# Score matmuls in row tiles with masks moved off TensorE, one ring of four PSUM banks, and value products issued for two steps together

## The chip, the cores and the metric

One core of one Trainium2 chip. The metric is device time in microseconds (us) of one execution, as the median of a few runs; lower is better.

## What is computed

Input x is 4 batches x 1024 tokens x 128 features, all fp32. Two blocks follow each other, both with 16 heads of 8 features:

```python
x = x + layernorm(attn(layernorm(x)))          # causal attention with ALiBi bias
x = x + layernorm(ffn(layernorm(x)))           # full attention, then a mixture of experts

def attn(x, Wq, bq, Wk, bk, Wv, bv, Wo, bo):
    q, k, v = heads(x @ Wq + bq), heads(x @ Wk + bk), heads(x @ Wv + bv)   # 16 heads x 8
    scores = einsum('bhqd,bhkd->bhqk', q, k) * 8 ** -0.5
    scores = scores + slopes[:, None, None] * (qpos - kpos)
    scores = where(kpos <= qpos, scores, -inf)
    return einsum('bhqk,bhkd->bqhd', softmax(scores), v) @ Wo + bo

def ffn(x, ...):
    x = x + layernorm(attention(x), ln1)       # no bias on the scores, no mask
    return x + layernorm(moe(x), ln2)          # 8 experts, top 2, hidden 512, gelu
```

## The kernel before, in words

`build` runs five stages: a row pass `first` (layernorm, transposes, values), the causal attention `at1`, a row pass `second`, the full attention `at2`, and `tail` (output projection, norms, experts). Both attentions are the function `attention` (L206) with another `Plan` (L56). The change lies there; in `build` only constants change.

**Slots.** An attention works in 16 slots, one for a batch and a group of four heads. The four heads lie side by side in the 128 partitions, 32 rows each: 24 rows hold the 8 features three times over (high and low parts, since fp32r keeps fewer bits), the rest bias and maximum rows. `fq` is the query side. `km` is the key side with four copies, one for each head, in which the rows of the other three heads are zero, so that a 128-row matmul gives one head's scores.

**Streams of a slot** (names as in the code):
- `proj`, 4 a slot, three slots ahead: three matmuls (a fourth for the causal bias) into the bank `misc`; ScalarE reads it into `u` (L404); GpSimd splits it (`hi` L556, `part` L559, then `fq` L564 or `fk` L567 and the four masked copies `km` L569). In the first slot VectorE does this.
- `a`: scores with queries on the partitions, only for each row's maximum. A chunk is 128 queries by up to 512 keys (L333), for several heads at once where the causal width is under 512. In the causal attention a chunk on the diagonal gets a second matmul that adds the mask (L337). VectorE reduces the bank by maximum (L466). Three banks.
- `m`, `mtr`: VectorE joins the maxima (L474 to L481), TensorE transposes them into `misc` (L346), VectorE adds them to the queries, `fqm` (L486).
- `b`: scores with keys on the partitions, maximum taken off (L360), with a mask matmul on the diagonal (L363). ScalarE takes exp into `probs` (L415). Three banks.
- `pv`: four matmuls with 32 columns each, one a head, side by side in the array, accumulate values and row sums in the bank `pv` (L378); `oev` copies it out (L420), `otr` transposes it back (L385), VectorE divides (L492, L494).

**Order.** One list, made by `Plan.body` for a slot, is walked by all engines. It has a step for each quad (512 queries x 128 keys x 4 heads): 12 quads in the causal attention, 16 in the other. A step holds four `b`, about four `a` between them, at times a `proj`, `mtr` or `otr`, and the `pv` of the quad before. TensorE issues in this order, so whatever it waits for holds everything behind it. `a` works a slot ahead of `b`. The loop runs over three batches with four slots in its body; four slots and a prologue are written out.

## Time and profile before

| | |
|---|---|
| median of 3 runs | 2289.69 us (2287.66 to 2295.19) |
| profiled execution, first to last instruction | 2287.5 us; the lowest run is 0.2 us above it |
| TensorE busy | 2102.9 us (92%), 11100 matmuls |
| VectorE busy | 1671.8 us (73%) |
| ScalarE busy | 1373.5 us (60%) |
| GpSimd busy | 977.3 us (43%) |
| mean granted TensorE clock | 0.959 |

A granted clock of 1.00 is 2.4 GHz, 0.50 is 1.2 GHz. Busy time of TensorE is the union of matmul spans; matmuls are pipelined, so a span (0.4 us for 512 columns) is longer than the distance between two starts. Distances between starts are what counts.

### The profile page before, as it was taken

The numbers are of one execution on the slowest core, as the hardware profiler recorded it, in microseconds if no ns is written. First come the engines' busy times: TensorE is split into PE (matmuls) and PEld (weight loads), VectorE is DVE, ScalarE is ACT, GpSimd is POOL, SyncE is SP. The second block draws the span as 40 slices with busy tenths as digits, with TensorE's granted clock in tenths as the row PEclk, the third lists the DMA queues.
The fourth block names the chain that finished last, engine by engine and source line by source line (L and its number), as shares of the span: only waits on it lengthen the run. The fifth ranks groups of instructions, "written<-read, shape, count | busy, mean of one in ns | idle before, by whom it ended". The sixth has DMA issues, their size and how long they took to land. (4 is left out here: it accounts for less than half of the span.)

```text
span 2287.5 us, 41083 instructions
## 1 busy us (share of the span) xinstructions
PE 2102.9 (92%) x11100; PEld 1223.1 (53%) x11100; DVE 1671.8 (73%) x3157; ACT 1373.5 (60%) x2647; POOL 977.3 (43%) x744
## 2 busy tenths in 40 slices
PE   5899999999999679999999999999993999999996
PEld 4455555555554534555555555555531666666664
DVE  5766667666672787777777777778822899998986
ACT  4266566666666616666666666666672655555654
POOL 3665464553610355333333333342002466565554
PEclk7799999999999679999999999999996999999998
DMA  2000000000000300000000000000001100000000
GB/s 59 1 2 1 3 1 1 2 2 1 1 1 2 110 0 1 2 1 1 2 1 1 2 1 1 1 1 1 1 1 61 51 19 19 2 19 19 19 10 10
DMA packets 27508, 24.96 MB, mean 11 GB/s; under 512 B 2409, under 2 KB 21110, under 8 KB 27282
## 3 DMA queue, kind: packets, MB, share of 16 engines
q1 hardware_dynamic: 26400, 21.91, 3.2%
q8 instruction: 103, 1.69, 0.3%
q14 instruction: 123, 1.01, 0.2%
q10 hardware_dynamic: 882, 0.36, 0.1%
HBM read 13.87 MB, written 6.29 MB: 9 GB/s over the span
## 5 line engine op out<-in xcount | busy, mean ns | idle before, releaser
L466 DVE TENSOR_REDUCE at_mx<-at_a 128x1 f32<-128x512 f32 (+3 forms) x1632 | 1010.8, 675 | 358.7 <-PE at_a L333 249.5
L415 ACT ACTIVATE at_probs<-at_b 128x512 f32<-128x512 f32 (+3 forms) x1792 | 888.6, 558 | 474.0 <-PE at_b L360 292.7
L333 PE MATMUL at_a<-at_km,at_fq 128*128 128x512 f32 (+1 forms) x1632 | 704.8, 439 | 20.4 <-DVE at_mx L466 9.8
L360 PE MATMUL at_b<-at_fqm,at_km 128*128 128x512 f32 (+3 forms) x1792 | 710.8, 404 | 11.4 <-ACT at_probs L415 7.6
L333 PEld LDWEIGHTS at_a<-at_km,at_fq 128*128 128x128 f32 x1632 | 316.3, 194 | 290.0 <-DVE at_mx L466 224.4
L360 PEld LDWEIGHTS at_b<-at_fqm,at_km 128*128 128x128 f32 x1792 | 339.8, 191 | 205.5 <-ACT at_probs L415 120.3
L378 PE MATMUL at_pv<-at_probs,at_vst 128*32 128x512 f32 (+3 forms) x3584 | 437.9, 561 | 1.5 <-ACT at_probs L415 1.5
L556 POOL TENSOR_TENSOR at_hi<-at_u,split_sign 128x512 fp32r<-128x512 f32 x120 | 124.9, 1041 | 441.1 <-ACT at_u L404 306.5
L1172 ACT ACTIVATE t_hid<-t_bank_h,b1t 128x512 f32<-128x512 f32 x256 | 174.3, 689 | 195.9 <-DVE t_hid_lo L1306 113.1
L1306 DVE TENSOR_TENSOR t_hid_lo<-t_hid,t_hid_hi 128x512 fp32r<-128x512 f32 x256 | 225.6, 917 | 15.0 <-ACT t_hid_hi L1179 11.8
L569 POOL TENSOR_TENSOR at_km<-at_fk,head_mask 128x2048 fp32r<-128x2048 f32 x60 | 216.1, 3602 | 11.2 <-POOL at_fk L567 11.0
L1340 POOL TENSOR_TENSOR t_hid_hi<-t_hid,pow_cols 128x512 fp32r<-128x512 f32 x112 | 141.1, 1275 | 129.6 <-ACT t_hid L1172 129.0
L404 ACT ACTIVATE at_u<-at_misc,bias 128x512 f32<-128x512 f32 x128 | 88.2, 689 | 124.7 <-PE at_misc L203 58.0
L526 POOL COPY at_vst<-tokens 128x256 f32 (+1 forms) x32 | 13.0, 405 | 328.5 <-PE at_pv L378 328.2
L201 PE MATMUL t_bank_y<-t_hid_hi,t_w2hi 128*128 128x512 f32 x256 | 106.6, 416 | 31.3 <-DVE t_weighed L1315 26.8
L559 POOL TENSOR_TENSOR at_part<-at_hi,split_sign 128x512 f32<-128x512 f32 x120 | 125.0, 1042 | 21.4 <-POOL at_hi L556 21.4
L378 PEld LDWEIGHTS at_pv<-at_probs,at_vst 128*32 128x32 f32 x3584 | 70.6, 108 | 117.1 <-ACT at_probs L415 85.1
L363 PE MATMUL at_b<-ident,causal_mask 128*128 128x128 bf16 x512 | 117.8, 232 | 0.0
L203 PE MATMUL t_bank_y<-t_hid_hi,t_w2lo 128*128 128x512 f32 x256 | 102.2, 399 | 0.0
L202 PE MATMUL t_bank_y<-t_hid_lo,t_w2hi 128*128 128x512 f32 x256 | 101.9, 398 | 0.0
L337 PE MATMUL at_a<-causal_mask,ident 128*128 128x128 bf16 (+2 forms) x352 | 91.7, 260 | 0.0
L564 POOL TENSOR_TENSOR at_fq<-at_part,at_u 128x512 fp32r<-128x512 f32 x60 | 77.0, 1284 | 10.7 <-POOL at_part L559 10.7
(211 smaller groups left out, 2410.3 us busy)
## 6 DMA issues: line engine op xcount, KB each, us to landing
t_raw<-L_ffn_W SPq DMA_DIRECT2D x16, 256.0 KB, 3.1
x_first<-L_attn_x SPq DMA_DIRECT2D x4, 512.0 KB, 7.3
second_x_in<-L_attn_x SPq DMA_DIRECT2D x8, 256.0 KB, 3.1
kept<-second_joined SPq DMA_DIRECT2D x8, 256.0 KB, 2.6
kept_u<-second_normed SPq DMA_DIRECT2D x8, 256.0 KB, 2.0
t_heads_in<-tokens SPq DMA_DIRECT2D x8, 256.0 KB, 2.6
t_u_in<-kept_u SPq DMA_DIRECT2D x8, 256.0 KB, 3.1
t_x_in<-kept SPq DMA_DIRECT2D x8, 256.0 KB, 3.1
```

The costliest lines, as they stand in the source:

```text
L333: mm = pe.matmul(scores, fq[g][:, qt * P:(qt + 1) * P], km[g][:, heads[0]:heads[0] + k, kh * HALF:kh * HALF + w], start=True, stop=not dia ...
L360: mm = pe.matmul(out[:, 0:w], km[g][:, j, kt * P:(kt + 1) * P], fqm[g % 2][:, q0:q0 + w], start=True, stop=not diagonal)
L363: mm = pe.matmul(out[:, 0:P], causal_mask[:, :], ident16[:, :], start=False, stop=True)
L378: mm = pe.matmul(pv_bank[HW * j:HW * (j + 1), HALF - w:HALF], vst[g % 2][:, kt, j, :], probs[(n % 2) * GH + j][:, 0:w], start=(kt == 0), s ...
L415: act.activation(probs[(t % 2) * GH + j][:, 0:w], b_bank[n % 3][:, 0:w], ACT.Exp).then_inc(exp_done, 1)
L466: dve.tensor_reduce(mx[:, kh, qt, heads[0]:heads[0] + k], a_bank[n % 3][:, 0:k * w].rearrange("p (k w) -> p k w", k=k), AX.X, ALU.max).the ...
L556: pool.tensor_tensor(hi[:, :], un[:, :], split_sign[:, 2:3].broadcast_to([P, HALF]), ALU.add).then_inc(pool_step, 1)
L559: pool.tensor_tensor(part[:, :], hi[:, :].bitcast(F32), split_sign[:, m:m + 1].broadcast_to([P, HALF]), ALU.mult).then_inc(pool_step, 1)
L569: pool.tensor_tensor(km[g][:, :, half], fk[:, None, :].broadcast_to([P, GH, HALF]), head_mask[:, :, None].broadcast_to([P, GH, HALF]), ALU ...
L1172: act.activation(hid[:, f, :], h_bank[f][:, :], ACT.Gelu, bias=b1t[:, f, e:e + 1]).then_inc(hidden["act"], 1)
L1306: dve.tensor_tensor(hid_lo[e % 2][:, f, :], hid[:, f, :], hid_hi[e % 2][:, f, :].bitcast(F32), ALU.subtract).then_inc(hidden["dve"], 1)
L1340: pool.tensor_tensor(out, a, b, op).then_inc(stage["pool"], 1)
```

## The change

- Instead of four masked copies of the keys there is one, `fk`. A score matmul contracts only the 32 rows of its head, so it uses one of four row groups of the array. `a` and `b` matmuls alternate, and `b` takes the heads in the order 2, 3, 0, 1 (`b_head`), so that neighbours use different row groups.
- The mask matmuls go. In `a`, a chunk is one head; on the diagonal ("ragged": 32 of 48 causal chunks) VectorE adds a row mask and takes the maximum in one call. In `b`, exp runs over unmasked scores, and GpSimd then sets the upper triangle of 4 x 128 columns to zero for the quads on the diagonal; `pv` waits for that.
- `a` has four banks, and `proj`, `otr` and `mtr` use the same ring instead of `misc`.
- `pv` of two quads is issued together, ahead of every second step, from four sets of `probs` instead of two.

```diff
+RING = ("a", "proj", "otr", "mtr")
+A_BANKS = 4
+B_BANKS = 3
+PROBS = 4
...
-                per = max(1, HALF // n)
-                per = 4 if per >= 4 else per
-                for j in range(0, GH, per):
-                    self.chunks.append((qt, kh, list(range(j, j + per)), n))
+                for j in range(GH):
+                    self.chunks.append((qt, kh, j, n))
+
+        self.ragged = [i for i, (qt, kh, j, n) in enumerate(self.chunks) if causal and kh * HALF + n == (qt + 1) * P]
...
-        o0 = self.half_end[0] + 3 - self.lead
+        o0 = self.half_end[0] + 1
...
         for i in range(self.nq):
+
+            for p in (i - 1, i) if i % 2 else ():
+                out.append(("pv", 0, p))
+                if p in self.half_end:
+                    out.append(("oev", 0, self.half_end.index(p)))
             q = i + self.lead
...
-            dp, p = (ds, q - 1) if q else (0, self.nq - 1)
-            if dp == 0 or do_a1:
-                out.append(("pv", dp, p))
-                if p in self.half_end:
-                    out.append(("oev", dp, self.half_end.index(p)))
         return out
+
+    def places(self, steps):
+
+
+        order = [step for step in steps if step[0] in RING]
+        return {step: place for place, step in enumerate(order)}
...
+def b_head(n):
+
+
+    return (n + 2) % GH
...
@@ TensorE @@
+                def bank_free(step):
+
+                    place = places[step] - A_BANKS
...
-                        mm = pe.matmul(scores, fq[g][:, qt * P:(qt + 1) * P],
-                                       km[g][:, heads[0]:heads[0] + k, kh * HALF:kh * HALF + w],
-                                       start=True, stop=not diagonal)
-                        if diagonal:
-                            mm = pe.matmul(scores[:, :, w - P:w], ident16[:, :],
-                                           causal_mask[:, None, :].broadcast_to([P, k, P]),
-                                           start=False, stop=True)
+                        rows = slice(HW * j, HW * (j + 1))
+                        mm = pe.matmul(misc[:, 0:w], fq[g][rows, qt * P:(qt + 1) * P],
+                                       fk[g][rows, kh * HALF:kh * HALF + w],
+                                       start=True, stop=True)
...
-                        mm = pe.matmul(out[:, 0:w], km[g][:, j, kt * P:(kt + 1) * P],
-                                       fqm[g % 2][:, q0:q0 + w], start=True, stop=not diagonal)
-                        if diagonal:
-                            mm = pe.matmul(out[:, 0:P], causal_mask[:, :], ident16[:, :],
-                                           start=False, stop=True)
+                        out = b_bank[n % B_BANKS]
+                        rows = slice(HW * j, HW * (j + 1))
+                        mm = pe.matmul(out[:, 0:w], fk[g][rows, kt * P:(kt + 1) * P],
+                                       fqm[g % 2][rows, q0:q0 + w], start=True, stop=True)
...
+                        if n in plan.diagonals:
+                            done(pe, masked, len(plan.diagonals), s, plan.diagonals.index(n))
...
@@ ScalarE @@
-                        if j == 0:
-                            done(act, pv_done, NQ, s, t - 2)
+                        if n % GH == 0:
+                            done(act, pv_done, NQ, s, t - PROBS)
...
@@ VectorE @@
+                        if n in plan.ragged:
+                            ragged = plan.ragged.index(n)
+                            if ragged >= 2:
+                                done(dve, a_read, NA, s, plan.ragged[ragged - 2])
+                            dve.sem_inc(dve_passed, 1)
+                            dve.tensor_tensor_reduce(scrap[ragged % 2][:, 0:w], scores, causal_rows[:, HALF - w:HALF], 1.0,
+                                                     -3.0e38, ALU.add, ALU.max,
+                                                     mx[:, kh, qt, j:j + 1]).then_inc(a_read, 1)
+                        else:
+                            dve.tensor_reduce(mx[:, kh, qt, j:j + 1], scores, AX.X, ALU.max).then_inc(a_read, 1)
...
@@ GpSimd @@
+                    if what == "b" and n % GH == GH - 1 and n // GH in plan.diagonals:
+                        await_(exp_done, NB, s, n)
+                        block_ = probs[n // GH % PROBS][:, :, 0:P]
+                        pool.affine_select(block_, block_, [[0, GH], [1, P]], ALU.is_ge, 0.0, base=0,
+                                           channel_multiplier=-1).then_inc(masked, 1)
...
-                        pool.tensor_tensor(fk[:, :], part[:, :], un[:, :], ALU.add).then_inc(pool_step, 1)
-                        await_(pool_step, count, s, step + 2)
-                        pool.tensor_tensor(km[g][:, :, half],
-                                           fk[:, None, :].broadcast_to([P, GH, HALF]),
-                                           head_mask[:, :, None].broadcast_to([P, GH, HALF]),
-                                           ALU.mult).then_inc(split_done, 1)
+                    dst = fk if m else fq
+                    pool.tensor_tensor(dst[g][:, half], part[:, :], un[:, :], ALU.add).then_inc(split_done, 1)
```

How this moves the instructions. First TensorE in `at2`, in the loop, around a value product; "ISA" stands for a register or wait instruction. Before:

```order
L333 MATMUL at_a<-at_km,at_fq 128x512
L265 ISA
L360 MATMUL at_b<-at_fqm,at_km 128x512
L265 ISA
L378 MATMUL at_pv<-at_probs,at_vst 32x512 x4
L265 ISA
L333 MATMUL at_a<-at_km,at_fq 128x512
L265 ISA
L360 MATMUL at_b<-at_fqm,at_km 128x512
```

and now:

```order
L367 MATMUL at_a<-at_fk,at_fq 128x512
L289 ISA
L390 MATMUL at_b<-at_fqm,at_fk 128x512
L289 ISA
L407 MATMUL at_pv<-at_probs,at_vst 32x512 x4
L289 ISA
L407 MATMUL at_pv<-at_probs,at_vst 32x512 x4
L289 ISA
L367 MATMUL at_a<-at_fk,at_fq 128x512
L289 ISA
L390 MATMUL at_b<-at_fqm,at_fk 128x512
```

Two groups of value products stand in a row, and the next such pair comes two steps later.

VectorE in `at1`, in the loop, among the `a` reductions. Before, three chunks, the middle one of four heads:

```order
L466 TENSOR_REDUCE at_mx<-at_a 128x1
L265 ISA
L466 TENSOR_REDUCE at_mx<-at_a 128x4
L265 ISA
L466 TENSOR_REDUCE at_mx<-at_a 128x1
```

and now, a full chunk and a ragged one with its two instructions at L497 (the second writes the maximum, `at_mx`):

```order
L501 TENSOR_REDUCE at_mx<-at_a 128x1
L289 ISA x2
L497 ISA at_scrap,at_mx<-at_a,causal_rows 128x256
L497 ISA at_mx 128x1
L289 ISA x2
L497 ISA at_scrap,at_mx<-at_a,causal_rows 128x256
```

A diagonal chunk has become one chunk a head, each with one instruction more.

GpSimd in `at1`, in the loop, from the staging of the values. Before:

```order
L526 COPY at_vst<-tokens 128x32x8
L265 ISA x3
L556 TENSOR_TENSOR at_hi<-at_u,split_sign 128x512
L265 ISA
L559 TENSOR_TENSOR at_part<-at_hi,split_sign 128x512
L265 ISA
L567 TENSOR_TENSOR at_fk<-at_part,at_u 128x512
L265 ISA
L569 TENSOR_TENSOR at_km<-at_fk,head_mask 128x4x512
```

and now:

```order
L562 COPY at_vst<-tokens 128x32x8
L289 ISA
L580 AFFINE_SELECT at_probs<-at_probs 128x4x128
L289 ISA
L580 AFFINE_SELECT at_probs<-at_probs 128x4x128
L289 ISA x3
L597 TENSOR_TENSOR at_hi<-at_u,split_sign 128x512
L289 ISA
L600 TENSOR_TENSOR at_part<-at_hi,split_sign 128x512
L289 ISA
L605 TENSOR_TENSOR at_fk<-at_part,at_u 128x512
```

The product for `km` is gone, and masks of the probabilities stand in front of and between the splits.

## Rows read from the trace of the kernel before

**Rows 1.** Windows of `at2`: busy us and count of each engine, clock, DMA share, GB/s
```profile
1000.00:1200.00 200.00, 197.66 (x1034) 106.78 (x1031) 154.51 (x270) 135.36 (x254) 74.86 (x54) 0.99 0.01 2
```
**Rows 2.** Timeline, GpSimd, L526, once a slot: start us, duration us, instruction, idle before
```profile
187.86 0.40 POOL L526 COPY at_vst<-tokens 128x256 f32 x1 [5.98 <-PE at_pv L378]
228.51 0.40 POOL L526 COPY at_vst<-tokens 128x256 f32 x1 [6.00 <-PE at_pv L378]
...
1200.20 0.40 POOL L526 COPY at_vst<-tokens 128x256 f32 x1 [12.55 <-PE at_pv L378]
1254.28 0.40 POOL L526 COPY at_vst<-tokens 128x256 f32 x1 [12.56 <-PE at_pv L378]
```
**Rows 3.** Timeline of `at2`, one step and an output piece
```profile
1303.41 1.06 PE L378 MATMUL at_pv<-at_probs,at_vst 128*32 128x512 f32 x8
1304.41 0.50 PE L333 MATMUL at_a<-at_km,at_fq 128*128 128x512 f32 x1
...
1304.94 3.08 DVE L466 TENSOR_REDUCE at_mx<-at_a 128x1 f32<-128x512 f32 x5 [0.40 <-PE at_a L333]
...
1305.26 1.58 ACT L415 ACTIVATE at_probs<-at_b 128x512 f32<-128x512 f32 x3 [1.41 <-PE at_b L360]
...
1305.91 0.88 PE L333 MATMUL at_a<-at_km,at_fq 128*128 128x512 f32 x2
...
1306.62 0.39 PE L360 MATMUL at_b<-at_fqm,at_km 128*128 128x512 f32 x1
1306.94 1.06 PE L378 MATMUL at_pv<-at_probs,at_vst 128*32 128x512 f32 x8
...
1309.90 0.60 PE L385 MATMUL at_misc<-ident,at_osb 128*128 128x128 f32 x4
...
1310.87 0.25 DVE L492 RECIPROCAL at_rec<-at_misc 128x16 f32<-128x16 f32 x1
1311.32 0.29 DVE L494 TENSOR_TENSOR tokens<-at_misc,at_rec 128x128 f32 x1 [0.19 <-DVE at_rec L492]
```
**Rows 4.** Timeline of `at1`: the maximum's chain, a masked `b`, a narrow value product
```profile
509.80 0.36 DVE L474 TENSOR_TENSOR at_mfull<-at_mx 128x32 f32<-128x32 f32 x1 [0.32 <-DVE at_mx L466]
...
511.39 1.88 DVE L466 TENSOR_REDUCE at_mx<-at_a 128x4 f32<-128x512 f32 x3
...
516.33 0.48 PE L360 MATMUL at_b<-at_fqm,at_km 128*128 128x512 f32 x1
...
516.69 0.42 PE L333 MATMUL at_a<-at_km,at_fq 128*128 128x384 f32 x1
...
519.28 0.42 PE L378 MATMUL at_pv<-at_probs,at_vst 128*32 128x128 f32 x8
519.63 0.45 PE L360 MATMUL at_b<-at_fqm,at_km 128*128 128x384 f32 x1
```
**Rows 5.** Groups by line and form: count, busy us, mean ns, idle us before
```profile
L466 DVE TENSOR_REDUCE at_mx<-at_a 128x1 f32<-128x512 f32 x1408 | 881.9, 685 | 295.4 <-PE at_a L333 249.5 <-PE at_a L337 44.5 <-issue 0.6
L415 ACT ACTIVATE at_probs<-at_b 128x512 f32<-128x512 f32 x1408 | 744.1, 604 | 346.1 <-PE at_b L360 292.7 <-PE at_b L363 49.3
...
L569 POOL TENSOR_TENSOR at_km<-at_fk,head_mask 128x2048 fp32r<-128x2048 f32 x60 | 216.1, 3602 | 11.2 <-POOL at_fk L567 11.0
...
L556 POOL TENSOR_TENSOR at_hi<-at_u,split_sign 128x512 fp32r<-128x512 f32 x120 | 124.9, 1041 | 441.1 <-ACT at_u L404 306.5 <-PE at_b L360 124.8 <-POOL at_km L569 8.7
...
L466 DVE TENSOR_REDUCE at_mx<-at_a 128x1 f32<-128x384 f32 x128 | 70.4, 557 | 42.7 <-PE at_a L337 39.5
...
L486 DVE TENSOR_TENSOR at_fqm<-at_fq,at_misc 128x512 fp32r<-128x512 f32 x64 | 43.6, 682 | 11.7 <-PE at_misc L346 10.7
```
**Rows 6.** Windows: the prologue of `at2` twice, then the last slot of `at2`
```profile
820.00:830.00 10.00, 9.38 (x22) 4.89 (x21) 9.20 (x17) 1.38 (x2) 4.97 (x4) 0.78 0.01 2
830.00:840.00 10.00, 8.74 (x23) 4.14 (x23) 10.00 (x18) 1.38 (x2) 8.75 (x8) 1.00 0.00 1
...
1700.00:1710.00 10.00, 9.02 (x49) 3.63 (x52) 0.00 (x0) 8.30 (x17) 0.00 (x0) 1.00 0.00 0
```

More of the change, by code:

```diff
@@ L76, in __init__ @@
                 self.quads.append((qh, kt))
+        self.diagonals = [t for t, (qh, kt) in enumerate(self.quads) if causal and kt * P >= qh * HALF]
         self.na = len(self.chunks)
@@ L234, in attention @@
         rec = sb("rec", [P, HQ, GH])
-        a_bank = [bank(f"a{i}") for i in range(3)]
-        b_bank = [bank(f"b{i}") for i in range(3)]
+        a_bank = [bank(f"a{i}") for i in range(A_BANKS)]
+        b_bank = [bank(f"b{i}") for i in range(B_BANKS)]
         pv_bank = bank("pv")
-        misc = bank("misc")
+        in_body = plan.places(plan.body())
+        in_prologue = plan.places(plan.prologue())
+        assert len(in_body) % A_BANKS == 0
         proj_made = sem("proj_made")
@@ L261, in attention @@
         o_done = sem("o_done")
+        masked = sem("masked")
         init = sem("init")
@@ L319, in emit @@
                     elif what == "a":
-                        qt, kh, heads, w = plan.chunks[n]
+                        qt, kh, j, w = plan.chunks[n]
                         _, g = where(b0, g0, ds)
@@ L394, in _, with emit @@
                 act.sem_inc(semaphore, per)
-            def emit(steps, s0, b0, g0):
+            def emit(steps, s0, b0, g0, places, before):
                 for what, ds, n in steps:
@@ L403, in emit @@
                         done(act, split_done, 4, s, n - 2)
+                        misc = a_bank[places[what, ds, n] % A_BANKS]
                         act.activation(u[n % 2][:, :], misc[:, :], ACT.Identity,
@@ L428, in _, with emit @@
                 dve.sem_inc(semaphore, per)
-            def emit(steps, s0, b0, g0):
+            def emit(steps, s0, b0, g0, places, before):
                 for what, ds, n in steps:
@@ L438, in emit @@
                         un = u[n % 2]
-                        own = 5 * h if m else 5 * h + 3
+                        own = 4 * h + 2 * (n % 2)
                         done(dve, proj_read, 4, s, n)
@@ L458, in emit @@
+                        dve.tensor_tensor(dst[g][:, half], part[:, :], un[:, :], ALU.add).then_inc(split_done, 1)
                     elif what == "a":
-                        qt, kh, heads, w = plan.chunks[n]
+                        qt, kh, j, w = plan.chunks[n]
                         done(dve, a_made, NA, s, n)
                         if n == 0:
-                            if steps[0] == ("proj", 0, 0) and type(b0) is int and ds == 0:
+                            if places is in_prologue and ds == 0:
@@ L484, in emit @@
                         done(dve, m_turned, 2, s, n)
+                        misc = a_bank[places[what, ds, n] % A_BANKS]
                         h = slice(n * HALF, (n + 1) * HALF)
@@ L488, in emit @@
                     elif what == "otr":
+                        misc = a_bank[places[what, ds, n] % A_BANKS]
                         turned = misc[:, :].rearrange("p (t j c) -> p t j c", t=HQ, j=GH)
@@ L504, in _ @@
         def _(pool):
-            for semaphore, per in ((split_done, 4), (v_staged, 1)):
-                pool.sem_inc(semaphore, per)
+            for semaphore, per in ((split_done, 4), (v_staged, 1), (masked, len(plan.diagonals))):
+                if per:
+                    pool.sem_inc(semaphore, per)
             pool.memset(mpad[:, :, :], 0.0).then_inc(init, 1)
@@ L527, in stage_values, with emit @@
                                  src.rearrange("p t (j c) -> p t j c", j=GH)).then_inc(v_staged, 1)
-            def emit(steps, s0, b0, g0):
+            def emit(steps, s0, b0, g0, places, before):
                 if steps[0][1] == 0 and steps[0][0] == "proj":
@@ L532, in emit @@
                 else:
-                    if any(k[0] == "pv" and k[1] == 1 for k in steps):
+                    if any(k[0] == "b" and k[1] == 1 for k in steps):
                         b, g = where(b0, g0, 1)
@@ L547, in emit @@
                         first = False
-                    if type(b0) is int and steps[0] == ("proj", 0, 0) and ds == 0:
+                    if places is in_prologue and ds == 0:
                         continue
```

124 lines of the change are left out of this document (56 added, 68 removed).

## The prediction

> **What bounds the kernel now.** I read the page first, then the attention stages by windows (which engine is next), by the one instruction that comes once a slot (its length), and by the timeline of single steps (the distances from which the loops are built). The page puts TensorE at 92% of the span. In a stretch of the second attention it is busy 197.7 of 200 us at a granted clock of 0.99, VectorE 154.5, ScalarE 135.4 [rows 1]: the next engine is only a fifth away.
>
> The length of one pass of the loop (a slot: one batch, four heads) comes from the staging copy on GpSimd, once per slot: 187.86 to 228.51, so 40.65 us in the causal attention, and 1200.20 to 1254.28, so 54.08 us in the other [rows 2]. Each attention has 16 slots, about 650 and 865 us. Everything else (prologues, row passes, expert stage) is changed little.
>
> Timeline of a step [rows 3]. A group of value products of four heads starts at 1303.41, the next score matmul at 1304.41: 1.00 us. With 128 columns instead of 512 the same distance is 0.35 us (519.28 to 519.63, [rows 4]), so a group costs 0.13 us plus 1.69 ns a column. Five reductions in a row last 3.08 us, one alone 0.685 [rows 5]: 0.60 from each to the next. Three exps last 1.58, one 0.604: 0.49. From an `a` matmul's start to its reduction 0.53 us (1304.41 to 1304.94); I take the same from `b` to exp. The fifth `a` of a step starts at 1306.39 (1305.91 + 0.88 - 0.40); the second reduction ended at 1306.22: 0.17 us from a freed bank to its next matmul. The next matmul, the last `b`, follows 0.23 us behind it at 1306.62, the pace of score matmuls of 512 columns; the value products follow 0.32 behind that.
>
> **The change, part by part.** (1) *Masks off TensorE.* 54 per causal slot, 32 behind `b` and 22 behind `a`. A masked 512-column matmul takes 0.36 us to the next instead of 0.23 (516.33 to 516.69, [rows 4]); with 54 of them, 7 us a slot of TensorE. It goes to two places.
>
> (1a) VectorE: each of the 32 ragged chunks of a causal slot becomes a fused add and maximum plus a second instruction that writes the result. Add and maximum should take what the reduction takes: the two-input operation on PSUM for `at_fqm` has the same 682 ns as the reduction's 685 [rows 5]. The second instruction is in no row. Below: nothing, if it hides in the chain. Above: 0.25 us, the reciprocal of 16 elements [rows 3]. The other small operations of this chain stand between these, so I take 0.15. 32 x 0.15 = 4.8 us a slot.
>
> (1b) GpSimd zeroes the upper triangle of 4x128 probabilities for 8 of 12 steps. Bounds: 1.04 us (its cheapest 512-element operation) to 3.6 us (the `at_km` product) [rows 5]. I take 1.3, nearest the first since the element count is that. It runs a step ahead of the value products, so it is hidden; if GpSimd is late the value products wait, and both score streams behind them in TensorE's queue (rival E).
>
> (2) *`at_km` goes*: 3.6 us on GpSimd twice a slot, hidden in the bodies (it idles 441 us before `at_hi` [rows 5]), worth perhaps 8 us in the prologues, where splits are awaited.
>
> (3) *One head a chunk.* The causal slot has 48 chunks instead of 38, same columns. A reduction of 384 columns takes 557 ns against 685 for 512 [rows 5], so 0.13 us less per 128 columns: 0.60, 0.47, 0.34 and 0.22 us for 512 to 128. VectorE, causal slot: 16 full x 0.60 = 9.6; 8 x (0.60+0.47+0.34+0.22) = 13.0; second instructions 4.8. Other work: two `at_fqm` 1.2, the maximum's chain 1.9 (509.80 less its wait to 511.39, [rows 4]), two output pieces of 0.75 (1310.87 to 1311.61, [rows 3]): 4.6. Sum 32.0 us. Other attention: 64 x 0.60 + 4.6 = 43.0 us.
>
> (4) *Row tiles, four banks, value products in pairs.* Neighbouring matmuls now use different rows of the array. If they run side by side, TensorE stops being the bound and the ring of banks is. Follow eight chunks between two pairs of value products. From the start of reduction 4: 0.68 until its bank is free, 0.17 to matmul `a8`, 0.23 to `b8`, 0.32 to the value products, 1.00 + 0.87 for the pair, 0.53 to the next reduction: 3.80 us. VectorE has work for 5 x 0.60 = 3.00 of it. So it starves 0.80 us a pair: 8 x 0.60 + 0.80 = 5.6 us for two steps. ScalarE's loop over three `b` banks is 0.60 + 0.17 + 0.32 + 1.87 + 0.23 + 0.53 = 3.72 against 4 x 0.49: 1.76 idle, 5.68 us a pair. Two loops of equal length. Eight pairs are 44.8; with the 4.6 of other work **49.4 us** against 54.1: 16 x 4.7 = 75 us saved. Causal slot: the value products are 1.65, 0.78, 1.87, 1.87, 1.65 and 0.78 us; the same sum gives starvation of 0.6, 0, 0.8, 0.8, 1.5 (narrow chunks and the maximum's chain stand before it) and 0: 3.7. 32.0 + 3.7 + 0.5 for coupling = **36.2 us** against 40.65: 16 x 4.45 = 71 us.
>
> Tiling is also switched more often: four projections and four groups of transposes a slot now stand among row tiles. In the rows a switch from 128x128 to the 32-column products costs about 0.1 us (0.32 less the last matmul's 0.23), so 8 x 2 x 0.1 = 1.6 us a slot of TensorE's time, inside its slack. The Trainium skill, TensorEngine Tiling (Array Packing), Key Properties, says that changing the mode drains the array; by it alone these switches would speak against the change, and if each cost a whole matmul of 0.5 us they would take 8 us a slot. The measured 0.1 us is what such a drain costs here, and even 8 us would fit under 49.4.
>
> (5) *Last slots.* Slots 15 and 16 have few or no `a`. There a step now takes 2.4 us (49 matmul records in 10 us, 12 a step, [rows 6]). ScalarE's loop without `a8` and `a1` is 5.4 us a pair, 2.7 a step. Some 25 steps x 0.3 = 8 us lost, which cancels (2).
>
> **Sum:** 2287.5 - 75 - 71 = 2141.5. The profiled execution's span is 2287.5; the median of the three runs is 2.2 above it, so about **2144 us** for a run.
>
> **The rivals.**
>
> *B: row tiles don't overlap.* For it: each still loads weights of 128 columns, and every matmul has a wait in front. TensorE: eight pairs of 16 x 0.23 + 1.87 + 0.1, i.e. 8 x 5.65 = 45.2; projections 12 x 0.23 = 2.8; 16 transposes of 0.15 (four last 0.60 [rows 3]), 2.4; switches 1.6: 52.0 us a slot, saving 2.1. Causal slot: 33 us of TensorE, below VectorE but close, so about 37.5, saving 3.1. 16 x 5.2 = 83: **2206 us**. The Trainium skill, TensorE: Matmul & The Clock Gate, "Measured speedup vs the span model", gives 3.07x for four row tiles; by it 16 matmuls would take an estimated 1.2 us instead of 3.7 and B falls, but no run here shows it.
>
> *C: overlap shortens the loops too.* If `b8` runs beside `a8` and a result needs less than 0.53 us, starvation halves to 0.4: 3.2 and 1.8 us a slot less, 16 x 5 = 80: **2064 us**.
>
> *D: the clock falls (slower).* TensorE now pauses for a bank after almost every matmul. The nearest stretch is the prologue of the second attention, where VectorE is the bound: 22 matmuls in 10 us with a granted clock of 0.78, then 23 in the next ten with 1.00 [rows 6]: mixed. At 1.2 GHz a pair of value products lasts 1.74 us more and `b8` 0.2: 1.9 x 8 = 15 us a slot, 64.9 us instead of 54.1; causal, the products' 7.8 us double and part is hidden, some 42: 16 x (10.8 + 1.4) = 195 above now, **2485 us**. It decides from a share of time at 1.2 GHz of 0.43 (146 of 341), a mean clock of about 0.78 over the attention stages. Against it: the value products still fill a third of the time, and 200 us with a loop's end in them keep 0.99 [rows 1]. The Trainium skill, TensorE: Matmul & The Clock Gate, "A second HAM failure mode: psum-queue depth-cycling", tells of just this: short idles between groups that cycle through banks make the clock swing between its levels. The prologue agrees in part.
>
> *E: GpSimd's masks come late.* A split (1.04 + 1.04 + 1.28 us and waits) stands between two masks in steps 6 and 7. If a mask takes 3.6 us, four pairs a slot wait about 1 us: +64, **2208 us**.
>
> **How the numbers follow.** Forecast (A) 0.50, B 0.18, C 0.15, D 0.13, E 0.04. The likeliest gives 2144; its own range is 2067 to 2195 from the second instruction alone (-77 to +51). The range 2050 to 2290 takes in B, E, nearly all of C and the mild part of D, and leaves out some 0.17. A measurement of this kernel can tell 0.3% from no change: 7 us. A, B, C and E are all faster; of D 0.11 is slower by more than that, 0.01 within it and 0.01 faster, and 0.01 of B (some clock lost as well) lies within it: faster 0.87, same 0.02, slower 0.11.
>
> **What would show it.** Staging copies 36.2 and 49.4 us apart; the granted clock at 0.95 or more; VectorE with one wait of about 0.8 us per pair of value products and otherwise busy; matmul starts of an `a` and its neighbour `b` under 0.1 us apart (B: 0.23); the second instruction at 0.15 us; value products waiting on GpSimd nowhere. Copies over 54 us apart with a clock below 0.8 would make D right; a TensorE without pauses and 52 us, B.

## The result and the profile after

The changed kernel took **2540.64 us** (median of 4, 2527.02 to 2551.51) against 2288.68 us for the kernel before, measured beside it: 1.109 times as long, 95% interval 1.104 to 1.114. The forecast was 2144 us and faster. The profiled execution, the fastest of the four, spans 2525.3 us, 237.8 more than before. Ratios here and below are of fast executions alone; one run each of x4, x6 and x9, over 1.5% above the fastest of its kernel, is in the times given for it but not in the ratio.

The windows of the two attentions, of the changed kernel (columns as in [rows 1]: busy us and count of TensorE, its weight loads, VectorE, ScalarE, GpSimd; then the clock):

```profile
250.00:700.00 450.00, 405.36 (x2030) 182.88 (x2029) 254.18 (x822) 217.30 (x495) 174.47 (x194) 0.64 0.01 1
1100.00:1600.00 500.00, 457.72 (x2243) 176.44 (x2247) 331.49 (x586) 287.89 (x555) 110.55 (x104) 0.77 0.01 1
```

The granted clock, 0.99 in [rows 1], is 0.64 in the causal attention and 0.77 in the other. Short windows of the second show which two levels make up the 0.77:

```profile
1370.00:1375.00 5.00, 5.00 (x22) 1.73 (x21) 2.18 (x4) 2.13 (x4) 1.28 (x2) 0.50 0.00 0
1385.00:1390.00 5.00, 4.67 (x29) 2.20 (x29) 4.92 (x9) 4.27 (x9) 1.82 (x2) 1.00 0.01 2
1395.00:1400.00 5.00, 5.00 (x26) 1.23 (x24) 1.52 (x4) 0.14 (x2) 0.00 (x0) 0.50 0.00 0
1410.00:1415.00 5.00, 4.34 (x33) 1.60 (x32) 4.25 (x9) 3.11 (x7) 0.00 (x0) 1.00 0.00 0
```

1.2 GHz and 2.4 GHz alternate. At the low level TensorE is busy for 5.00 of 5 us and VectorE for 2.18 and 1.52, at the high one TensorE for 4.67 and 4.34 and VectorE for 4.92 and 4.25. The staging copies of the changed kernel, one a slot, which answer to [rows 2]:

```profile
397.61 0.40 POOL L562 COPY at_vst<-tokens 128x256 f32 x1
446.18 0.40 POOL L562 COPY at_vst<-tokens 128x256 f32 x1
...
1343.22 0.40 POOL L562 COPY at_vst<-tokens 128x256 f32 x1 [17.88 <-PE at_pv L407]
1407.96 0.40 POOL L562 COPY at_vst<-tokens 128x256 f32 x1 [16.25 <-PE at_pv L407]
1469.32 0.40 POOL L562 COPY at_vst<-tokens 128x256 f32 x1 [16.26 <-PE at_pv L407]
```

The causal slot shown takes 48.6 us (they range from 44.4 to 54.7 in the loop; 40.65 before), one of the other attention 64.7 and 61.4 in turn (54.1 before). From the first to the sixteenth copy the causal attention takes 720.4 us against 627.0, the other 931.9 against 828.3: 93.4 + 103.6 = 197 of the 238 us. Another 11 lie between the attentions and some 31 behind the last copy, where the last slot runs at a clock of 0.70.

The timeline of the changed kernel across a change of the clock (it answers to [rows 3]):

```profile
1404.30 3.35 PE L407 MATMUL at_pv<-at_probs,at_vst 128*32 128x512 f32 x16
...
1407.58 0.50 PE L367 MATMUL at_a<-at_fk,at_fq 32*128 32x512 f32 x1
...
1407.58 0.50 PE L390 MATMUL at_b<-at_fqm,at_fk 32*128 32x512 f32 x1
...
1407.59 0.49 PE L367 MATMUL at_a<-at_fk,at_fq 32*128 32x512 f32 x1
...
1407.59 0.72 PE L390 MATMUL at_b<-at_fqm,at_fk 32*128 32x512 f32 x2
...
1408.11 2.48 DVE L501 TENSOR_REDUCE at_mx<-at_a 128x1 f32<-128x512 f32 x4 [2.18 <-PE at_a L367]
...
1411.81 1.93 PE L407 MATMUL at_pv<-at_probs,at_vst 128*32 128x512 f32 x16
1413.66 0.50 PE L367 MATMUL at_a<-at_fk,at_fq 32*128 32x512 f32 x1
```

Three things are read here. Row tiles do run side by side: four matmuls start within 10 ns. The pair of value products takes 3.28 us at 1.2 GHz (1404.30 to 1407.58) and 1.85 us a loop later at 2.4 GHz, and VectorE stands 2.18 us ahead of its next reduction. And at full clock the loop is nearly the forecast one: 6.08 us from 1407.58 to 1413.66 with four output transposes in it, against 5.6 without.

The groups of the changed kernel that answer to the unknown costs (with [rows 5]):

```profile
L407 PEld LDWEIGHTS at_pv<-at_probs,at_vst 128*32 128x32 f32 x3584 | 123.2, 146 | 315.9 <-issue 221.7 <-ACT at_probs L449 85.3 <-POOL at_probs L580 7.9
L497 DVE CUSTOM_DVE_ANT_0 at_scrap<-at_a,causal_rows 128x512 f32<-128x512 f32 x128 | 81.9, 687 | 65.3 <-PE at_a L367 65.3
L580 POOL TENSOR_SCALAR_AFFINE_SELECT at_probs<-at_probs 128x512 f32<-128x512 f32 x128 | 81.6, 640 | 314.5 <-ACT at_probs L449 314.5
...
L497 DVE DVE_READ_ACCUMULATOR2_ANT at_mx<- 128x1 f32 x512 | 42.4, 83 | 0.0
```

Add and maximum take 687 ns, as the reduction; the second instruction 83 ns, the mask on GpSimd 640 ns. The value products' weight loads wait 7.9 us for it in all.

### The profile page after: what moved, and what is told of

It reads as the page before. It is cut to its first block and busy times, and to the rows that moved or that the text cites. A ratio compares the mean times of both kernels' runs of the same rounds, so it can differ in the third digit from the quotient of the medians.

```text
span 2525.3 us, 41740 instructions
## 1 busy us (share of the span) xinstructions
PE 2210.6 (88%) x10396; PEld 1080.9 (43%) x10396; DVE 1659.5 (66%) x3824; ACT 1329.2 (53%) x2647; POOL 837.5 (33%) x812
## 5 line engine op out<-in xcount | busy, mean ns | idle before, releaser
L501 DVE TENSOR_REDUCE at_mx<-at_a 128x1 f32<-128x512 f32 x1280 | 789.0, 683 | 324.3 <-PE at_a L367 322.7
L390 PE MATMUL at_b<-at_fqm,at_fk 32*128 32x512 f32 (+3 forms) x1792 | 687.2, 547 | 91.5 <-ACT at_probs L449 90.7
L367 PE MATMUL at_a<-at_fk,at_fq 32*128 32x512 f32 (+3 forms) x1792 | 599.5, 533 | 54.0 <-DVE at_mx L501 20.9
L407 PE MATMUL at_pv<-at_probs,at_vst 128*32 128x512 f32 (+3 forms) x3584 | 617.9, 830 | 2.7 <-POOL at_probs L580 2.7
L367 PEld LDWEIGHTS at_a<-at_fk,at_fq 32*128 32x128 f32 x1792 | 269.3, 226 | 397.9 <-issue 206.5
L390 PEld LDWEIGHTS at_b<-at_fqm,at_fk 32*128 32x128 f32 x1792 | 290.9, 219 | 319.8 <-ACT at_probs L449 262.5
L497 DVE CUSTOM_DVE_ANT_0 at_scrap<-at_a,causal_rows 128x384 f32<-128x384 f32 (+3 forms) x512 | 232.9, 488 | 237.5 <-PE at_a L367 229.5
L580 POOL TENSOR_SCALAR_AFFINE_SELECT at_probs<-at_probs 128x512 f32<-128x512 f32 x128 | 81.6, 640 | 314.5 <-ACT at_probs L449 314.5
L438 ACT ACTIVATE at_u<-at_a,bias 128x512 f32<-128x512 f32 x128 | 88.0, 687 | 171.5 <-PE at_a L222 112.3
L220 PE MATMUL at_a<-turned_hi,w_hi 128*128 (+1 forms) x128 | 83.4, 652 | 10.7 <-PEq L642 5.8
```

Source lines behind the costliest of these rows:

```text
L220: pe.matmul(out, a[0], b[0], start=start, stop=False)
L367: mm = pe.matmul(misc[:, 0:w], fq[g][rows, qt * P:(qt + 1) * P], fk[g][rows, kh * HALF:kh * HALF + w], start=True, stop=True)
L390: mm = pe.matmul(out[:, 0:w], fk[g][rows, kt * P:(kt + 1) * P], fqm[g % 2][rows, q0:q0 + w], start=True, stop=True)
L407: mm = pe.matmul(pv_bank[HW * j:HW * (j + 1), HALF - w:HALF], vst[g % 2][:, kt, j, :], probs[n % PROBS][:, j, 0:w], start=(kt == 0), stop= ...
L497: dve.tensor_tensor_reduce(scrap[ragged % 2][:, 0:w], scores, causal_rows[:, HALF - w:HALF], 1.0, -3.0e38, ALU.add, ALU.max, mx[:, kh, qt, ...
L501: dve.tensor_reduce(mx[:, kh, qt, j:j + 1], scores, AX.X, ALU.max).then_inc(a_read, 1)
```

## The experiments

The question was why the clock is low: is it idle time (rival D's reason), or something in the matmuls themselves? In each text below, "Theory" and "Rival" are what was expected before that kernel ran.

**x1_full_rows** and **x4_one_group** change only which rows a score matmul contracts. x1, in the second attention (its scores are sums over four heads, so the attention's values are others):

```diff
-                        rows = slice(HW * j, HW * (j + 1))
+                        rows = slice(HW * j, HW * (j + 1)) if causal else slice(0, P)
```

> The changed kernel, but in the second attention every score matmul contracts all 128 rows of fk and fq (so it sums the scores of four heads; its output is not the reference's). No two score matmuls can then run side by side. The causal attention is unchanged. Theory 1 (the clock falls because a score matmul fills only 32 of 128 rows): granted clock 0.97 or more in the second attention, slot 52 us (eight pairs of 16 x 0.23 + 1.87 + 0.1, plus projections and transposes), total about 2527 - 16 x 11 = 2350. Theory 2 (it falls because overlapped score matmuls leave TensorE idle between banks): the same, since TensorE then has no idle time. Theory 3 (it falls because of the ring or the pairs of value products, whatever the matmuls are): clock stays near 0.79, slot 60 us or more.

x4, in both attentions (every head's scores are taken from the first head's rows):

```diff
-                        rows = slice(HW * j, HW * (j + 1))
+                        rows = slice(0, HW)
```

> The changed kernel, but every score matmul uses rows 0 to 31 (all four heads get the scores of the first; its output is not the reference's). The matmuls still fill 32 rows, but must follow each other, 0.23 us apart, as before the change. Theory 1 (few rows filled): clock stays below 0.85 in both attentions, slots of the second attention 62 us or more. Theory 2 (idle time between banks): clock 0.97 or more, slots of 52 us in the second attention and 38 in the causal one, total about 2220.

x1 took 2353.9 us (2347.11 to 2360.69), 1.029 times the kernel before (1.025 to 1.033). x4's two runs took 2789.75 and 2832.51 us; the first is 1.22 times the kernel before. Windows of x1, then of x4, with two short ones:

```profile
1000.00:1600.00 600.00, 589.29 (x3211) 342.63 (x3212) 475.21 (x840) 413.27 (x792) 155.99 (x146) 0.99 0.01 2
```

```profile
1100.00:1800.00 700.00, 693.37 (x2774) 353.00 (x2771) 422.10 (x723) 372.91 (x682) 132.58 (x125) 0.73 0.00 1
...
1515.00:1530.00 15.00, 15.00 (x87) 7.80 (x79) 11.52 (x19) 10.08 (x19) 5.42 (x5) 1.00 0.00 1
1550.00:1580.00 30.00, 30.00 (x87) 16.71 (x86) 16.04 (x27) 13.47 (x23) 3.35 (x3) 0.50 0.00 0
```

x4 decides against idle time: TensorE works 693.4 of 700 us and the clock is still 0.73. From 1515 to 1530 us it works without a gap at the full clock, and from 1550 to 1580 us, again without a gap, the clock is 0.50. Most slots take 70 to 77 us, as its first theory expected (62 or more). Its score matmuls have the rows of one head; x1, with 128 rows and the same order, ring and pairs, is at 0.99, and its slots are 51.8 to 52.0 us, as expected. The values in x1 and x4 are not the reference's; that they make the difference is unlikely, since x12 below computes the reference with 128 rows and pairs, and is at 0.99 too.

**x13_half_rows** stands between the two: 64 rows in the second attention (sums over two heads).

```diff
-                        rows = slice(HW * j, HW * (j + 1))
+                        rows = slice(HW * j, HW * (j + 1)) if causal else slice(2 * HW * (j // 2), 2 * HW * (j // 2 + 1))
```

> The changed kernel, but the score matmuls of the second attention contract 64 rows (two heads summed), so that they use one of two row groups; everything else, the order and the switches between row tiles and whole-array work too, stays. It stands between the changed kernel (32 rows: slots of 61 to 65 us, granted clock 0.77) and x1_full_rows (128 rows: 52 us, 0.99). Theory 'it is the number of rows at work that sets the clock': the clock lies between, 0.85 to 0.95 in 1100 to 1600 us, slots of 54 to 59 us, total 2410 to 2500. Rival 'it is the switching between row tiles and the whole array, or any row group at all, whatever its height': clock 0.75 to 0.80 and slots of 61 us or more, total about 2540.

One run of 2372.55 us. The same window of x13:

```profile
1100.00:1600.00 500.00, 479.79 (x2722) 219.59 (x2722) 399.89 (x709) 345.24 (x671) 134.22 (x126) 0.99 0.01 2
```

Neither number was right: 64 rows already keep 0.99, with slots of 51.0 us. But the rival falls: alternating row groups, pairs and switches are all there, and the height of a score matmul (with it, how many can run side by side) is what the edit changes against the changed kernel's 0.77. TensorE's pauses are there too, though shorter (479.8 of 500 us busy against 457.7); that pauses are not needed for the low clock was x4's result. These 51.0 us are also what the changed kernel's order gives at full clock, with two row groups side by side instead of four; the forecast was 49.4.

**x6_single** keeps 32 rows and issues the value products one step at a time.

```diff
-            for p in (i - 1, i) if i % 2 else ():
+            for p in (i,):
```

> The changed kernel with one thing undone: value products of one step at a time (those of quad i at the head of step i), instead of pairs every second step. Theory 1 alone (32-row matmuls keep the clock down, the pairs are innocent): clock stays near 0.77 in the second attention, slot 60 us or more. Theory 1 with the pairs (with pairs TensorE has 4 us stretches of row tiles only, and falls there; single value products come every 3 us and keep the clock up, as in the warm slots of x2_row_tiles): clock 0.9 or more in the second attention; ScalarE's loop is 0.60 + 0.17 + 0.32 + 1.00 + 0.23 + 0.53 = 2.85 us a step, slot 16 x 2.85 + 3.3 = 49 us where the clock is full, 49 to 53 on average; causal slot 36 to 41. Total 2140 to 2240, below both kernels.

It took 2373.66 us (2350.72 to 2392.25), ratio 1.040 (1.035 to 1.045). Windows of x6:

```profile
250.00:750.00 500.00, 439.55 (x2287) 174.15 (x2288) 296.53 (x928) 249.07 (x560) 188.47 (x212) 0.63 0.01 1
1000.00:1600.00 600.00, 501.73 (x3316) 184.22 (x3312) 494.52 (x866) 427.81 (x816) 157.94 (x149) 0.98 0.01 2
```

Half as expected. In the loop of the second attention the clock is back at 0.98, with TensorE idle *more* (501.7 of 600 us busy), and slots are 50.0 to 50.4 us: there it takes both the few rows and the pairs to lower it. In the causal attention it stays at 0.63 without any pair, with slots of 44 to 54 us (36 to 41 were expected), and the total is above 2140 to 2240. Why the pairs matter in one attention and not in the other is not shown.

**x2_row_tiles** and **x5_masks_off** each make one half of the change to the kernel before. x2 has the row tiles alone; mask matmuls stay between them:

```diff
-                        mm = pe.matmul(out[:, 0:w], km[g][:, j, kt * P:(kt + 1) * P],
-                                       fqm[g % 2][:, q0:q0 + w], start=True, stop=not diagonal)
+                        rows = slice(HW * j, HW * (j + 1))
+                        mm = pe.matmul(out[:, 0:w], fk[g][rows, kt * P:(kt + 1) * P],
+                                       fqm[g % 2][rows, q0:q0 + w], start=True, stop=not diagonal)
```

> The kernel before with the row tiles alone: one fk, 32-row score matmuls, one head a chunk, heads of b in the order 2, 3, 0, 1; masks stay on TensorE, three banks for each stream, the fourth for misc, value products singly. Theories 1 and 2: the clock falls in the second attention, where no mask matmul fills the array, to 0.7 to 0.85, slot above 54.1 us, about 58. Theory 3 (ring or pairs to blame): clock 0.97 or more there and slots of 50 us or less, since VectorE's 43 us are then the bound with waits for exp.

x2 took 2969.14 us (2958.41 to 2979.87), ratio 1.298 (1.292 to 1.303). Its windows:

```profile
300.00:1400.00 1100.00, 1088.20 (x3774) 456.87 (x3778) 374.27 (x744) 357.73 (x726) 151.86 (x144) 0.53 0.00 1
1500.00:2200.00 700.00, 593.94 (x3458) 229.22 (x3461) 542.98 (x944) 449.76 (x843) 189.98 (x178) 0.91 0.01 1
```

and a piece of its causal timeline:

```profile
702.31 0.58 PE L331 MATMUL at_a<-at_fk,at_fq 32*128 32x256 f32 x1
...
702.82 0.29 PE L335 MATMUL at_a<-causal_mask,ident 128*128 128x128 bf16 x1
...
703.04 0.47 PE L359 MATMUL at_b<-at_fqm,at_fk 32*128 32x128 f32 x1
```

Row tiles without the rest are the worst of all: 84.8 us for most causal slots, 1088 of 1100 us busy at 0.53. Each of the 64 masks of a slot (one for each head here, behind `a` and behind `b`) breaks a run of row tiles, so that little overlaps and every mask brings two switches of the array's shape. In the second attention, which has no masks, slots are 52 us with the clock at 1.00 (1610 to 1662) and 58 where it is lower (0.85 over 1662 to 1720). Neither expectation gave this mixture. It has 32 rows, single value products and a mean clock of 0.91, so single value products do not make the clock safe.

x5 has the masks off TensorE, and 128 rows:

```diff
-                        if diagonal:
-                            mm = pe.matmul(out[:, 0:P], causal_mask[:, :], ident16[:, :],
-                                           start=False, stop=True)
```

> The kernel before with the masks alone moved off TensorE (add and maximum on VectorE with one scrap buffer, zeroing on GpSimd, one head a chunk in the causal attention); 128-row score matmuls on km, three banks, value products singly. Every theory: clock 1.0, second attention unchanged at 54.1 us a slot. Causal slot: 54 masks x 0.13 = 7 us of TensorE gone, but VectorE's 32 us and GpSimd's (splits 15, km 7.2, masks 8 x 0.64) come nearer: 36 to 38 us against 40.65. Total 2289 - 16 x 3.5 = 2230, 2200 to 2260. A slot over 40 us would say that the masks were hidden, or that the value products now wait for GpSimd.

x5 took 2362.78 us (2360.33 to 2364.15), ratio 1.033 (1.031 to 1.034), a miss. Its waits in the causal attention, from 300 to 700 us (waited for: us in total, times, longest):

```profile
POOL at_probs L556 <- ACT at_probs L417: 127.4, 45, 6.1
...
DVE at_scrap L475 <- DVE at_mx L475: 37.7, 192, 0.5
...
PEld at_pv L380 <- POOL at_probs L556: 32.1, 23, 2.9
```

Causal slots go from 40.65 to 44.3 us although 54 mask matmuls are gone from each and only 10 more `a` chunks came. The value products, one step behind exp here, wait for GpSimd's masks (rival E's mechanism), VectorE for its own single scrap buffer, and the clock is 0.91; what each of the three costs is not separated. Even with 128 rows the masks' move was a loss in this order.

**x7_filler** and **x8_single_filler** try to buy the clock back: a matmul over 128 rows ahead of every second `b`, overwritten by that `b`; x8 has single value products as well.

```diff
+                        if n % 2 == 0:
+                            pe.matmul(out[:, 0:w], fk[g][:, kt * P:(kt + 1) * P],
+                                      fqm[g % 2][:, q0:q0 + w], start=True, stop=True)
```

> The changed kernel with more work: in front of every second b matmul, a full 128-row matmul into the same bank, which the real one then overwrites. If the low clock is what costs, more work makes it faster: clock 0.95 or more, pairs of steps 5.6 to 6.2 us instead of 7.7 (a filler costs 0.23 us and two switches of tiling), slot of the second attention 48 to 53, causal 40, total 2180 to 2300. If the time goes to something else (ring, GpSimd, switches), the fillers only add: 4 x 0.5 = 2 us a pair, slot 75 us, total 2800.

> x6_single and x7_filler together. Theory 1: clock 0.98 in both attentions; TensorE per step 1.0 + 2 x 0.5 + 8 matmuls of 0.1, under 3 us, so the slots are 50 us and 38, total 2150 to 2230. If x6_single alone already has the full clock, the fillers only cost and this one is slower than x6_single by 2 us a slot or more.

x7 took 2629.39 us (ratio 1.149, 1.145 to 1.153), x8 2566.03 (1.121, 1.117 to 1.125). The clock in 1200 to 1800 us rises to 0.91 and 0.97, yet slots stay at 62 us and more. For x7 that lies between its two theories (48 to 53, or 75 us); for x8, against the 50 us of x6 in this attention, it is the second one: the fillers only cost. The timeline of x7, at a clock of 1.00, shows the price:

```profile
1504.65 0.50 PE L367 MATMUL at_a<-at_fk,at_fq 32*128 32x512 f32 x1
1505.07 0.50 PE L391 MATMUL at_b<-at_fqm,at_fk 128*128 128x512 f32 x1
1505.50 0.50 PE L393 MATMUL at_b<-at_fqm,at_fk 32*128 32x512 f32 x2
```

From a row tile to the whole array 0.42 us, and 0.43 back, where equal shapes follow each other after 0.23: 0.2 us a switch, and the overlap is broken too.

**x9_split** puts together what had paid: causal attention of the kernel before, second attention of x6.

```diff
-        attention(nc, "at2", Plan(False), turned, tokens, tokens, w3[1], bias2[1], slope_rows, iota_rows,
-                  split_sign, head_mask, ident, ident16, causal_mask)
+        tiled_attention(nc, "at2", TiledPlan(False), turned, tokens, tokens, w3[1], bias2[1], slope_rows, iota_rows,
+                        split_sign, ident, None)
```

> The causal attention as before the change, the second attention as in x6_single (row tiles, ring of four banks, value products of one step). Theory 1: the two stages are independent, so the causal slot is 40.65 us at full clock, as before, and the other 50.0 us, as in x6_single: 2289 - 16 x 4.1 = 2223 us, 2210 to 2240, faster than both kernels. If the clock of the second attention had only held up by chance, its slots would be 53 us or more and the total 2270 or more.

2281.47 us (2267.81 to 2302.44), ratio 0.996 (0.991 to 1.0005): not told apart from no change. Its staging copies:

```profile
862.27 0.40 POOL L1028 COPY at_vst<-tokens 128x256 f32 x1
939.38 0.40 POOL L1028 COPY at_vst<-tokens 128x256 f32 x1 [13.67 <-PE at_pv L873]
989.62 0.40 POOL L1028 COPY at_vst<-tokens 128x256 f32 x1 [10.89 <-PE at_pv L873]
```

and windows of its prologue with most of the first slot, of that slot (the one that ends at 939.38), of a loop's end, and of the last slot:

```profile
820.00:920.00 100.00, 95.00 (x281) 38.01 (x281) 69.81 (x119) 34.03 (x60) 36.20 (x34) 0.50 0.00 1
...
862.00:939.00 77.00, 70.33 (x293) 23.54 (x291) 47.75 (x82) 38.94 (x73) 14.09 (x14) 0.58 0.00 1
...
1300.00:1320.00 20.00, 15.63 (x72) 4.91 (x72) 10.69 (x19) 9.25 (x18) 1.97 (x3) 0.66 0.02 4
...
1640.00:1700.00 60.00, 51.13 (x184) 13.38 (x183) 2.48 (x6) 29.17 (x57) 0.00 (x0) 0.50 0.00 1
```

The same code takes 50.2 us for a slot at full clock and 77.1 us at a mean of 0.58. From 820 to 920 us the clock is 0.50 with TensorE 95% busy; the kernel before, with 128 rows, has 0.94 in the same 100 us. The expectation's last sentence named a clock that had held up by chance, but its slots in the loop are those of x6; what is lost lies in the stretches shown.

**x10_a_masks** adds the `a` masks on VectorE to x9's causal attention and leaves the `b` masks on TensorE; **x11_fill_cold** adds fillers to x9's second attention where its clock was low:

```diff
+                        if n % 2 == 0 and (prologue or bare or (g0 == 0 and ds == 0 and n < 5 * GH)):
+                            pe.matmul(out[:, 0:w], fk[g][:, kt * P:(kt + 1) * P],
+                                      fqm[g % 2][:, q0:q0 + w], start=True, stop=True)
```

> x9_split, and in the causal attention the masks of the a stream alone moved to VectorE (one head a chunk, one scrap buffer); the masks of b stay on TensorE, GpSimd gets none. 22 masks x 0.13 us = 2.9 us a slot off TensorE, which stays the bound at 32 masks; VectorE's 32 us stay below it. If what made x5_masks_off slow was the wait of the value products for GpSimd, the causal slot is 38 to 40 us, clock 0.97 or more, total 2180 to 2215. If VectorE's longer chunks or a lower clock did it, the slot is 42 us or more and the total over 2240.

> This is x9_split (causal attention as before; second attention with row tiles, ring, GpSimd-free masks and value products of one step at a time) with extra full 128-row matmuls, whose results nobody reads, only where x9 showed a low clock: in the first slot of the second attention before every second a and b, in the first five quads of the slots at the head loop's start, and in slots without an a. Their results land in a PSUM bank that is overwritten anyway. Theory 'the few rows let the clock fall, and only these stretches are left of the loss': the first slot of the second attention goes from 77 us to 56 or less, the slots at the loop's ends from 55 to 58 to 52 to 54, the granted clock of 815 to 925 us is over 0.85, and the total is 2225 to 2260 us, under both kernels. Rival 'fillers cost as much as the clock gives back' (each adds its own time and two changes between row tiles and the full array at 0.2 us each, as in x7_filler): the first slot stays over 65 us and the total is 2290 us or more.

x10 took 2309.34 us, ratio 1.009 (1.005 to 1.012), with causal slots of 41.5 to 44.5 us at 0.95 and 49 at the loop's ends (44 before). That is its second branch: even without any mask on GpSimd the causal attention is slower than before, so GpSimd is not the whole reason for x5. x11 took 2285.95 us (11 runs), ratio 0.998 (0.997 to 1.000). The last slot's clock rises from 0.50 to 0.97, but over 815 to 925 us it is 0.58, the first slot still takes 71.8 us, and the intervals over the loop's ends are 61.3 and 66.5 us instead of 56.8 and 57.7. This is the side of its rival, with a total 4 us below the rival's.

How much the fillers did to the first slot, one trace each can't tell: x10 has the second attention of x9 unchanged, and there the slot took 61.7 us and not 77.1:

```profile
903.00:964.00 61.00, 52.97 (x291) 19.40 (x290) 47.07 (x82) 38.22 (x73) 13.58 (x13) 0.83 0.01 1
```

**x12_pairs_full** therefore gives up the row tiles and keeps the ring and the pairs in the second attention, with the four masked key copies; the fourth set of probabilities lies in memory that only the causal attention used. The causal attention is that of before.

```diff
-                        rows = slice(HW * j, HW * (j + 1))
-                        mm = pe.matmul(out[:, 0:w], fk[g][rows, kt * P:(kt + 1) * P],
-                                       fqm[g % 2][rows, q0:q0 + w], start=True, stop=True)
+                        mm = pe.matmul(out[:, 0:w], km[g][:, j, kt * P:(kt + 1) * P],
+                                       fqm[g % 2][:, q0:q0 + w], start=True, stop=True)
```

> Causal attention as before; the second attention keeps the four masked copies of the keys, so that its score matmuls contract all 128 rows, and takes from the change the ring of four banks and the value products of two steps in a row (with a fourth set of probabilities, in memory that only the causal attention needed). Unlike x1_full_rows it computes the reference. Theory 'rows, not pauses, set the clock; the rest of the change is worth 2 us a slot': as in x1_full_rows slots of 51.8 to 52.0 us in the loop against 54.1, a granted clock of 0.98 or more from 1000 to 1600 us, causal slots of 40.6, and no cold first slot (under 58 us; x9_split had 77.1). Total 2250 to 2265 us, faster than both kernels and than x9_split. Rival 'pairs of value products with their pauses lower the clock also in a kernel whose causal attention is warm, or x1's slots came from leaving the split of keys alone': slots of 54 us or more, a clock under 0.95, total 2285 us or more.

**2264.65 us** (2261.12 to 2265.78), ratio 0.989 (0.988 to 0.991): 1.1% faster than the kernel before, and the fastest of all. Windows and copies of x12:

```profile
250.00:700.00 450.00, 446.17 (x2917) 239.42 (x2914) 302.71 (x531) 279.23 (x589) 203.98 (x147) 0.99 0.01 2
...
1000.00:1600.00 600.00, 590.86 (x3223) 341.34 (x3221) 477.13 (x845) 415.66 (x797) 221.52 (x158) 0.99 0.01 1
```

```profile
1138.80 0.40 POOL L1028 COPY at_vst<-tokens 128x256 f32 x1 [12.21 <-PE at_pv L866]
1190.63 0.40 POOL L1028 COPY at_vst<-tokens 128x256 f32 x1 [12.21 <-PE at_pv L866]
```

Slots of 51.8 us against 54.1, and 53.1 us for the slot that took 77.1 in x9. Everything came as expected.

## Why the prediction was wrong

**The step that failed** is part (4), together with the argument against rival D: 49.4 and 36.2 us a slot were worked out at full clock, and the argument for full clock weighed TensorE's busy time (value products fill a third, [rows 1] keeps 0.99). The runs showed a clock of 0.77 and 0.64 in its place, and slots of 61.4 and 64.7 us and of 48.6. x4 shows that busy time does not keep the clock up here, and x1 and x13 that in the second attention the height of the score matmuls decides. The rows of before held no matmul on 32 rows, and no term asked what one is worth to the clock.

D had the right event, and by the prediction's own sign (copies over 54 us apart, clock below 0.8) it is the rival that came true, but its reason was pauses, which x4 lacks. That its sizes came near (64.9 us a slot; causal 42; 2485 us, measured 2540.64) is in part luck, because they stand for all the time at 1.2 GHz. A mean of 0.77 is 0.46 of the time, for which D's own sum gives 49.4 + 0.46 x 15.5 = 56.5 us, an estimate, and 63 were measured. D priced the low clock at 15 us a slot, for the value products and one `b`; x9's slot at 0.58 is 27 us longer than at full clock. At the low level TensorE is busy for 5.00 of 5 us and so is the bound again, which no term had. The share of 0.43 at which the change would break even is too high for the same reason.

The Trainium skill, TensorE: Matmul & The Clock Gate, "A second HAM failure mode: psum-queue depth-cycling", fits the swing between two levels in the trace after; that short idles between bank groups make it does not fit here, since x6 idles more at 0.98 and x4 hardly at all at 0.73.

What held and what did not, by the parts:

- (1a) The second instruction takes 83 ns, not 150: VectorE's term was 2.1 us a causal slot too large (32 x 0.067). Add and maximum cost what was said.
- (1b), rival E: the mask takes 640 ns, below the lower bound of 1.04. A pair of value products gives it time, and the wait is 7.9 us in all. E's place was right for x5, where value products follow a step behind exp.
- (4) Row tiles overlap, with starts under 0.1 us apart, so B falls; rival C too, since the loop at full clock is 6.08 us and not shorter. Of the forecast 4.7 us a slot, x13's 51.0 leaves 3.1 at full clock. Every loop of x13's slot at 1292 to 1343 us has a projection or transposes in it and lasts 6.1 to 6.6 us, those with a projection 6.3 to 6.6, though a projection gives VectorE nothing to do; this suggests that they lie on the path, not in TensorE's slack.
- Switches cost 0.2 us, twice the 0.1 that was read off the step into the 32-column products. At 16 a slot this is 1.6 us more, about the distance from 49.4 to 51.0; that all of that distance comes from them was not tried.
- (5) Last slots: 8 us were to be lost in all; behind the last copy alone it is 31, the last slot at a clock of 0.70.
- The causal slot of 36.2 us was never seen: no run had row tiles there at full clock. The nearest runs with 128 rows, x5 at 44.3 us (clock 0.91) and x10 at 41.5 to 44.5 (0.95), are both above the 40.65 of before. So whether the masks' move could pay in another order stays open, as does how much of the causal loss is clock.
- Open as well is why the first two intervals of x9's second attention last 134 us, at a low clock, when those of the changed kernel take 120, and those of x10, with the same code there, 119.

**The balance.** In the second attention three parts of the change act. Ring and pairs are worth 2.2 us a slot (x12: 54.1 to 51.9), and side-by-side matmuls about 1 more at full clock (x13: 51.0). With 32 rows and pairs the clock falls, which takes it all back and 7 to 11 us a slot besides. This accounts for some 104 of the 238 us; for the 93 us of the causal attention no run changed the height of the matmuls alone.

## What to carry to other kernels

Row tiles save array time but put few rows to work. Before splitting a contraction on an engine that is busy 90% of the time, ask what the granted clock will be afterwards, give a fall its full price in the forecast (all matmuls slower, TensorE the bound again), and look at the clock of the first run before anything else. Where several improvements come together, try them without the one that changes how full the array is: here the ring and the pairs alone made the faster kernel. And a switch between array shapes has a price of its own, so masks or fillers between row tiles cost more than their columns.

## What the runs showed of the hardware

- The granted clock depends on how many rows a matmul contracts. Second attention, same order and pairs: 0.77 with 32 rows, 0.99 with 64, 0.99 with 128; 32 rows one at a time, 0.73 at 99% busy. With 32 rows and single value products it was 0.98 in x6 and 0.91 in x2.
- Steady work does not end a low clock by itself: 0.50 over 820 to 920 us in x9 with TensorE 95% busy, and over 1550 to 1580 us in x4 with no gap.
- A matmul on 32 rows that overlaps with nothing takes as long as one on 128: 0.42 to 0.43 us from start to start in x4 at the low clock (1400.37 to 1401.23, two of them), and 0.43 for a projection's 128 rows there (1402.37 to 1402.80). A switch between row tiles and the whole array adds 0.2 us each way (0.42 and 0.43 us against 0.23).
- VectorE's accumulator read takes 83 ns; GpSimd zeroes the triangle of 512 columns in 640 ns, less than its 1.04 us for an addition of that size.
